# Delta-rule scan inside a decoder layer: key norms by a power on GpSimd, the output added by ScalarE and GpSimd, and another order of TensorE's work in each chunk

## What is computed

```python
proj = normed @ w_qkvb + b_qkvb
q, k, v, beta_pre = jnp.split(proj, 4, axis=-1)
beta = jax.nn.sigmoid(beta_pre)
# 16 heads of 16 features each
k = k / jnp.maximum(jnp.linalg.norm(k, axis=-1, keepdims=True), NORM_EPS)

def step(S, inp):
    q_t, k_t, v_t, beta_t = inp
    retrieval = jnp.einsum('bhij,bhj->bhi', S, k_t)
    S = S + jnp.einsum('bhi,bhj->bhij', beta_t * (v_t - retrieval), k_t)
    o_t = jnp.einsum('bhij,bhj->bhi', S, q_t)
    return (S, o_t)
_, out_t = lax.scan(step, S0, (q, k, v, beta))
return x + scan_out @ w_out + b_out
```

## Time and profile before

| | us |
|---|---|
| median of 3 runs | 1056.92 |
| the profiled execution | 1053.93 |
| its span in the profile | 1052.0 |
| PE busy | 909.3 (86%) |
| DVE busy | 876.4 (83%) |
| ACT busy | 656.4 (62%) |
| POOL busy | 516.5 (49%) |
| mean granted clock of TensorE | 0.937 of 2.4 GHz |

### The profile page before, as it was taken

The page is one execution under the profiler, slowest core; times in us unless marked ns, Lnnn a source line. Parts: engine busy times, 40 slices in busy tenths (PEclk is TensorE's granted clock), DMA queues, the critical chain, the costliest instruction groups (busy, mean ns, idle before and its releaser), DMA issues.

```text
span 1052.0 us, 19448 instructions
## 1 busy us (share of the span) xinstructions
PE 909.3 (86%) x6084; PEld 693.0 (66%) x6091; DVE 876.4 (83%) x2581; ACT 656.4 (62%) x1597; POOL 516.5 (49%) x753
## 2 busy tenths in 40 slices
PE   8799999999999999999999998989999901895066
PEld 7577787778778887877877877656666600442044
DVE  4789899989999999999999998865666657799887
ACT  4575777756667667666666665456777731894085
POOL 5344345433554563554355454236899980870000
PEclk9899999989999999999999999999999965898579
DMA  9700000000000000002100000132310000000012
GB/s 162 134 5 7 6 7 11 8 6 7 10 8 7 7 11 6 6 12 79 54 10 8 6 7 11 26 131 77 105 61 1 1 0 1 1 1 1 1 65 96
DMA packets 28573, 30.49 MB, mean 29 GB/s; under 512 B 5548, under 2 KB 23864, under 8 KB 28472
## 3 DMA queue, kind: packets, MB, share of 16 engines
q1 hardware_dynamic: 28256, 29.12, 11.0%
q10 hardware_dynamic: 216, 0.14, 0.0%
HBM read 20.85 MB, written 4.19 MB: 24 GB/s over the span
## 4 chain that ended last, share of the span: by engine, by line
PE 64%; DVE 17%; POOL 12%; issue 4%; ACT 1%; DMA 1%; SPq 1%; DVEq 0%; POOLq 0%; ACTq 0%
PE ps L1871 8%; PE ps L1863 7%; PE psG L1825 6%; PE ps L1802 5%; PE psY L1839 5%; PE psX L1839 4%; PE psX L1917 3%; PE psY L1917 3%; PE psG L1819 3%; PE ps L1931 2%; PE ps L2172 2%; PE psG L1820 2%; POOL arena L577 2%; POOL arena L575 2%; POOL xs L568 2%
## 5 line engine op out<-in xcount | busy, mean ns | idle before, releaser
L543 POOL TENSOR_TENSOR arena<-arena 128x256 f32<-128x256 f32 x32 | 23.3, 729 | 303.6 <-DVE arena L1206 303.6
L677 ACT ACTIVATE arena<-ps 128x512 f32<-128x512 f32 x128 | 72.9, 596 | 40.7 <-PE ps L1863 40.3
L1863 PE MATMUL ps<-work 32*128 32x256 f32 x512 | 94.2, 409 | 2.5 <-ACT work L723 1.8
L502 POOL TENSOR_SCALAR_AFFINE_SELECT arena<-arena 128x2048 f32<-128x2048 f32 x32 | 92.1, 2877 | 2.2
L642 ACT ACTIVATE arena<-ps,nparity 32x256 f32<-32x256 f32 x124 | 51.1, 458 | 48.3 <-PE ps L1802 47.9
L1863 PEld LDWEIGHTS ps<-work 32*128 32x128 f32 x512 | 62.7, 188 | 19.8 <-issue 12.0
L1825 PE MATMUL psG<-arena 128*128 128x512 f32 x128 | 74.0, 664 | 0.4 <-DVE arena L1272 0.4
L1217 DVE TENSOR_TENSOR arena<-arena 128x256 f32<-128x256 f32 (+1 forms) x96 | 66.6, 694 | 3.5
L1220 DVE TENSOR_REDUCE arena<-arena 128x64 f32<-128x256 f32 (+1 forms) x96 | 65.9, 686 | 3.3
L1802 PE MATMUL ps<-work,arena 128*128 128x64 f32 x496 | 61.5, 279 | 7.9 <-DVE work L1232 7.9
L1839 PEld LDWEIGHTS psY<-work,arena 128*128 128x128 f32 x512 | 59.8, 195 | 12.5 <-DVE arena L1289 10.7
(11 more groups left out here) (337 smaller groups left out, 2597.0 us busy)
## 6 DMA issues: line engine op xcount, KB each, us to landing
arena<-in_mask_BxSxS_ik SPq DMA_DIRECT2D x8, 1024.0 KB, 6.8
xs<-arena SPq DMA_DIRECT2D x256, 16.0 KB, 1.8
arena<-in_ctx SPq DMA_DIRECT2D x8, 512.0 KB, 4.4
out<-xs SPq DMA_DIRECT2D x32, 128.0 KB, 1.7
arena<-in_x SPq DMA_DIRECT2D x8, 288.0 KB, 17.9
arena<-in_L_ffn_w SPq DMA_DIRECT2D x2, 1024.0 KB, 21.9
arena<-in_x SPq DMA_DIRECT2D x16, 96.0 KB, 6.6
arena<-in_L_attn_w_qkvb SPq DMA_DIRECT2D x2, 512.0 KB, 5.2
```

The source lines that it names most:

```text
L502: G.affine_select(out=pairs, in_=pairs, compare_op=ALU.is_ge, fill=0.0, base=0, pattern=[[0, NH], [-CT, B], [0, CT]], channel_multiplier=1 ...
L677: A.activation(attn[j % 2][:, r * 512:(r + 1) * 512], ps[(2, 0)[r % 2]][:, :], ACT.Copy).then_inc(att_out, 1)
L1863: last = M.matmul(ps[(2, 0)[r % 2]][:, f * 2 * P:(f + 1) * 2 * P], kq[j % 4][rows, f * P:(f + 1) * P], qe[rows, f].rearrange("p e t -> p ( ...
```

## The change

1. VectorE's `key_norms` goes. ScalarE copies the sums of squares from PSUM to SBUF with the sign turned (`key_sums_out`), and GpSimd takes the maximum with the floor, raises it to the power -0.5 (`ALU.pow`, 128x16) and spreads it over the head's features with a copy.
2. VectorE's `x_added` goes. ScalarE copies the output projection from PSUM (`mixed_copied`, semaphore `mixed_out`), and GpSimd adds it to the chunk's input (`x_added`), after the masks and ahead of the norms. TensorE's waits for `x_done` become waits for `mixed_out`.
3. In `outputs` the loop over r, the strips of 32 columns, becomes the innermost.
4. TensorE's turn has a new order between the turned updates and the queries, as the last part of the diff shows.

```diff
-                ss, root, sqr = nrm
-                for n in range(3):
-                    own(G.tensor_tensor(sqr, root, root, ALU.mult))
-                    own(G.tensor_tensor(sqr, sqr, ss, ALU.mult))
-                    own(G.tensor_scalar(sqr, sqr, -0.5, 1.5, ALU.mult, ALU.add))
-                    if n < 2:
-                        own(G.tensor_tensor(root, root, sqr, ALU.mult))
+                ss, root, length = nrm
+                own(G.tensor_scalar(length, ss, NORM_EPS * NORM_EPS, None, ALU.max))
+                own(G.tensor_tensor(root, length, half, ALU.pow))
                 pool.wait_ge(rn_T, m)
-                wide = [t.rearrange("p (h a) -> p h a", a=1).broadcast_to([P, NH, HD]) for t in (sqr, root)]
-                G.tensor_tensor(rn_wide.rearrange("p (h d) -> p h d", d=HD), wide[0], wide[1], ALU.mult).then_inc(rn_ready, 1)
+                G.tensor_copy(rn_wide.rearrange("p (h d) -> p h d", d=HD),
+                              root.rearrange("p (h a) -> p h a", a=1).broadcast_to([P, NH, HD])).then_inc(rn_ready, 1)
+
+            def x_added(j):
+
+                pool.wait_ge(mixed_out, j + 1)
+                pool.wait_ge(xb_ready, j + 1)
+                G.tensor_tensor(xc[:, j, :], xc[:, j, :], mixed_s, ALU.add).then_inc(x_done, 1)
...
                 mask_attention(j)
+                if j >= 1:
+                    x_added(j - 1)
                 if j + 3 < NCK:
                     key_norms(j + 3)
...
+            def key_sums_out(m):
+
+                act.wait_ge(n_mm, m + 1)
+                act.wait_ge(rn_ready, m)
+                A.activation(nrm[0], ps[1][:, 0:NH], ACT.Copy, scale=-1.0).then_inc(seeded, 1)
+
+            def mixed_copied(j):
+
+                act.wait_ge(w_mm, j + 1)
+                act.wait_ge(x_done, j)
+                A.activation(mixed_s, ps[2][:, 0:D], ACT.Copy).then_inc(mixed_out, 1)
...
                     keys(m)
+                if exists(j - 1):
+                    mixed_copied(j - 1)
+                if exists(m):
+                    key_sums_out(m)
...
-            def key_norms(m):
-
-                v.wait_ge(n_mm, m + 1)
-                v.wait_ge(rn_ready, m)
-                ss, root, _ = nrm
-                squares, half = ps[1][:, 0:NH], ps[1][:, NH:2 * NH]
-                own(V.tensor_scalar(squares, squares, -1.0, NORM_EPS * NORM_EPS, ALU.mult, ALU.max))
-                own.issue(V.tensor_copy(ss, squares))
-                own(V.tensor_scalar(half.bitcast(I32), squares.bitcast(I32), 1, None, ALU.logical_shift_right))
-                own(V.tensor_scalar(root.bitcast(I32), half.bitcast(I32), -1.0, SEED, ALU.mult, ALU.add))
-                v.sem_inc(seeded, 1)
...
-            def x_added(j):
-                v.wait_ge(w_mm, j + 1)
-                v.wait_ge(xb_ready, j + 1)
-                V.tensor_tensor(xc[:, j, :], xc[:, j, :], ps[2][:, 0:D], ALU.add).then_inc(x_done, 1)
...
                     if j >= 1:
-                        pe.wait_ge(x_done, j - 1)
+                        pe.wait_ge(mixed_out, j - 1)
...
-                for r in range(4):
-                    for f in range(DC):
-                        for e in range(2):
+                for f in range(DC):
+                    for e in range(2):
+                        for r in range(4):
...
-                for f in range(2):
-                    if exists(j):
-                        attention(j, 2 * f)
-                        attention(j, 2 * f + 1)
-                    if exists(j + 1) and j >= 1:
-                        far_gram(j + 1, f)
-                    if f == 0 and exists(j + 2) and j >= 1:
-                        norms_turned(j + 2)
+                if exists(j + 1) and j >= 1:
+                    far_gram(j + 1, 0)
+                if exists(j):
+                    attention(j, 0)
+                    attention(j, 1)
+                if exists(j - 1):
+                    outputs(j - 1)
+                if exists(j):
+                    attention(j, 2)
+                    attention(j, 3)
+                if exists(j + 1) and j >= 1:
+                    far_gram(j + 1, 1)
+                if exists(j + 2) and j >= 1:
+                    norms_turned(j + 2)
                 if j == 0:
                     far_gram(1, 0)
                     far_gram(1, 1)
-                if exists(j - 1):
-                    outputs(j - 1)
```

More of the change, by code:

```diff
@@ L157, in decoder @@
         variances, newton = sums_of[:, 0:2, :], sums_of[:, 2:4, :]
-        half = sb("half", [P, B])[:, :]
+        half = sb("half", [P, NH])[:, :]
         w1q = sb("w1q", [P, FC, D], BF16)
@@ L213, in decoder @@
         nT += [take(D).rearrange("p (c t) -> p c t", c=DC) for _ in range(2)]
+        mixed_s = take(D)
         assert at[0] <= ARENA - NT * D, at[0]
@@ L358, in decoder @@
         yn_ready, hr_ready, hs_ready, tok_mm, picked, cand_ready = [sem(n) for n in "yn_ready hr_ready hs_ready tok_mm picked cand_ready".split()]
+        mixed_out = sem("mixed_out")
         last_known, att_moments, hid_moments, last_moments = [
@@ L532, in row_norms @@
                 own(G.tensor_scalar(qr[:, cols], s2[:, cols], 1.0 / D, LN_EPS, ALU.mult, ALU.add))
-                own(G.tensor_tensor(qr[:, cols], qr[:, cols], half, ALU.pow))
+                own(G.tensor_tensor(qr[:, cols], qr[:, cols], half[:, 0:B], ALU.pow))
                 G.tensor_tensor(qs[:, cols], qs[:, cols], qr[:, cols], ALU.mult).then_inc(q_known, 1)
@@ L551, in _ @@
                         bounded_weights(p)
+            x_added(NCK - 1)
             def beta_added(n):
@@ L938, in _ @@
                     scaled_by_feature(1)
+                    key_sums_out(0)
                 else:
                     normed_x(2 * m)
+                    key_sums_out(m)
                     scaled_by_feature(m + 1)
@@ L1178, in ternary_factors @@
                 v.wait_ge(abs_sum, 1)
+                v.wait_ge(seeded, 15)
                 own(V.tensor_reduce(wsum[:, :], ps[1][:, 32:40].rearrange("p (k n) -> p k n", k=2), AX.X, ALU.add))
@@ L1415, in _ @@
             input_stats(1)
-            key_norms(0)
             input_sums(1)
@@ L1421, in _ @@
             input_factors(1, input_total(1), -0.5)
-            key_norms(1)
             keys_normed(0)
@@ L1431, in _ @@
                 if j == 0:
-                    solve(0, {2: ((key_norms, 2),), 4: ((keys_normed, 1), (far_products, 1)), 8: ((near_products, 1),),
+                    solve(0, {4: ((keys_normed, 1), (far_products, 1)), 8: ((near_products, 1),),
                               12: ((keys_normed, 2),)})
@@ L1445, in _ @@
                     least(1)
-                if exists(j - 1):
-                    x_added(j - 1)
                 if exists(j + 1) and j + 1 < NCK - 1:
@@ L1451, in _ @@
                     state(j + 1)
-                if exists(j + 3):
-                    key_norms(j + 3)
                 if j == 11:
@@ L1928, in mixed @@
                 pe.wait_ge(oT_ready, j + 1)
-                pe.wait_ge(x_done, j)
+                pe.wait_ge(mixed_out, j)
                 for c in range(DC):
@@ L1947, in context_whole @@
                 else:
-                    pe.wait_ge(x_done, NCK - 1)
+                    pe.wait_ge(mixed_out, NCK - 1)
                 for u in range(NW):
@@ L1990, in probabilities @@
                 if n == 1:
-                    pe.wait_ge(x_done, NCK)
+                    pe.wait_ge(mixed_out, NCK)
                 elif n >= 2:
```

## The result

The changed kernel takes 1158.78 us (median of 4 runs, 1158.48 to 1159.43) where the kernel before takes 1056.02 in the same comparison: a ratio of 1.098, 95% interval 1.096 to 1.100. It is 10% slower. The forecast was 1147, slower.

A forecast was written before the change was run, and what follows sets the result against it. VectorE's ring and TensorE's order, nearly equal, were taken to hold the scan's 20.22 us turn. From 1053.93 us, +45.9 (wait for norms) and -1.3 gave 1098.5, +48.6 (slow clock) gave 1147; range 1090 to 1178.

The forecast's parts named there:

- What bounds the kernel: Scan loop over 32 chunks: VectorE's ring and TensorE's order of work, nearly equal, hold a turn of 20.22 us.
- VectorE's ring: Scan turn: VectorE's turned updates release the state's matmuls, then L1289, the retrieval, L1315 and the solve to the next updates.
- Part 1: Key norms and output addition leave VectorE: its ring gains 0.66 us a turn; ScalarE, GpSimd, prologue and tail cost nothing.
- Rival D: GpSimd's power takes over 6 us and becomes what L1228 waits for: 1150 us and up; chance 0.03.
- Part 2: TensorE's new order: turned norms end at 560.28 instead of 557.54, VectorE waits, a turn grows 1.70 us, +45.9 in 27 turns.
- rival C: TensorE's column groups don't run side by side, outputs stay 2.46 us: +34 us on top, 1132 or 1181; chance 0.08.
- Part 3: TensorE idles some 3.4 us ahead of every state, its clock halves: 1.8 us in each of 27 turns, +48.6.
- Rival B: VectorE's wait for the norms comes, but TensorE's clock stays at 2.4 GHz in most turns: about 1098 us; chance 0.16.
- The sum: Whole kernel: 1053.93 us plus 45.9 for the wait, less 1.3, gives 1098.5; plus 48.6 for the slow clock, 1147.
- Rival E: L1228 on VectorE isn't delayed; the ring gives 0.66 us in 31 turns, -20, so 1034 us; chance 0.05.

The follow-up runs named there:

- the moved work alone: Changed kernel with TensorE's order and the outputs' loop of the kernel before, so only key norms and output addition moved: 1049.14 us, ratio 0.994.
- the experiment on the tail: Changed kernel with GpSimd's addition of chunk 30 ahead of the masks of chunk 31 instead of behind them: 1151.07 us.
- the filled run: Changed kernel with 12 added 128x128 matmuls, read by nobody, ahead of every chunk's state on TensorE: 1096.44 us, ratio 1.039.
- the early norms: Changed kernel with TensorE turning the norms of chunk j + 2 right behind attention 0 and 1, ahead of the outputs: 1061.89 us, ratio 1.006.

## Why the prediction was right, and where it was off

**What bounds the kernel.** Right. Two chains of nearly equal length: with the moved work alone TensorE holds the turn at 20.2 us, with TensorE's order also relieved VectorE's ring goes to 19.66. The ring's gain of 0.66 us had been worked out, and 20.22 - 0.66 = 19.56 is 0.1 from what ran.

**Part 1.** Right in its terms. GpSimd in the turn shown above (L524 the addition, L515 the power, L517 the spread):

```profile
553.96 0.72 POOL L524 TENSOR_TENSOR arena<-arena 128x256 f32<-128x256 f32 x1
554.65 0.25 POOL L514 TENSOR_SCALAR work<-work 128x16 f32<-128x16 f32 x1
554.98 2.93 POOL L515 TENSOR_TENSOR work<-work,half 128x16 f32<-128x16 f32 x1
557.98 0.77 POOL L517 COPY work<-work 128x256 f32<-128x256 f32 x1
```

The power took 2.93 us (2.9 taken), and all ended at 557.98 + 0.77 = 558.75, while TensorE turned the norms at 564.11. Rival D falls. What was wrong is "The prologue and the tail change by less than 1 each way": for the tail I counted the added hop of the last addition, and not that the addition of the chunk before it now stood behind 5 us of masks in GpSimd's queue, nor that its transfers stood ahead of the last ones in SyncE's. This term was 7.8 us instead of 0, and the experiment on the tail took back 6.9 of it. It is two thirds of the 12 us between 1147 and 1159.

**Part 2.** Right in the mechanism, a little too high in size: +1.53 us a turn at full clock, measured with the filled idle time, instead of 1.70. Up to L1254 my order was right as a whole: from the first Gram to L1254 the filled run takes 538.55 to 544.31, 5.76 us, where I had 554.54 to 560.33, 5.79. Its pieces were off both ways: from the Gram to attention 0.95 instead of 1.06, the outputs 1.01 instead of 1.2 (rival C falls), attention 2 and 3 1.28 instead of 1.07. I had made attention 2 wait for both of ScalarE's copies; by the kernel it needs only the first (in the turn shown after, it starts at 561.87, ahead of the copies' end at 562.04), and attention 3 alone waits for the second. So that the errors cancel is luck. Most of the missing 0.17 lies behind L1254: the next state starts 8.38 us behind it (544.31 to 552.69) and not 8.52, since in the kernel before TensorE's own full queue held the state back a little: there it started 0.91 us behind L1232's start, here 0.77 behind L1258's.

**Part 3.** Right in the mechanism: idle time of 3.44 us (3.4 forecast) ahead of most states, half a clock behind it. The size was 2.15 us a turn instead of the middle of 1.8. From the ninth turn to the twenty-ninth every turn has a fall of 6.8 us or more, the longer of the two kinds that the earlier trace rows show; it costs less than the 3.0 us read there, and in the turn shown 1.4 of its 6.8 us pass while TensorE waits anyway (547.7 to 549.1). Rival B falls: the granted clock did fall. Without the slow clock the kernel would take 1096, as the filled run shows, which is B's 1098.

**The sum.** As forecast, the wait stands in 27 of the 29 turns; in the other two, at 89.2 and 227.8 us, VectorE starts L1254 without waiting. The filled run's 29 turns took 637.7 us, and this splits the stretch: the wait cost 637.7 - 599.1 = 38.6 us (45.9 forecast), the slow clock 697.4 - 637.7 = 59.7 (48.6 forecast). Together 98.3 against 94.5, because two errors of opposite sign nearly cancel. With the other rows of the table, -2.6, +1.5 and +7.8, for which I had 0, -1.3 and 0, it makes 105.0 against 93.2.

**Rival E**, no delay of L1228, is what the early norms make of the kernel. Its 1034 counted the ring's gain in every turn and no slow clock; 1061.9 was measured, since a relieved TensorE stands idle and the clock falls behind part of its waits. It takes added work or the slower outputs to collect the ring's gain, and even then 1043.2 was the best: the 29 turns gave 12.8 us back and the stretch behind them took 5.3.

## What to carry to other kernels

Before moving a producer in an in-order queue, look up where its consumer stands in its own queue, and compare the two times: here 1.09 us of slack in one row said that a step could be moved by one matmul group, not by four. When work moves to another engine, follow its last pass through every queue behind it: masks ahead of it on GpSimd and other transfers ahead of it on SyncE cost 7 us here that no turn of the loop shows. And where TensorE shares a ring with another engine, time saved on it beyond the ring's length is no gain and can be a loss by its clock: give it something to do, or leave it its slower loop.

## What the runs showed of the hardware that I had not expected

- 32 instructions of matmuls that fill strips of 32 columns took 1.08 us when each went to the next strip in turn, and 2.46 when all of one strip came before the next.
- Idle times of TensorE ahead of the state's matmuls, and the half clock: with 0.2 to 0.86 us it never came in these profiles; with 0.9 to 1.5 us it came in some turns and not in others of the same kernel, for 3.4 or 6.8 us (early norms: behind 0.90 at 317.3 and 1.39 at 519.8, not behind 1.02 at 297.6); with 2.0 to 2.6 us in most but not all (changed kernel: not behind 2.34 at 121.9 and 214.0); with 2.9 us and more in every turn.
- The slow clock hits the state's and the near Gram's matmuls in full (1.90 to 3.68 us; first part of the near Gram, from start to start, 0.92 to 1.82).
- Twelve matmuls a turn whose result nobody reads made the changed kernel 62 us faster.
- A power of 128x16 elements on GpSimd took 2.93 us, where 128x8 took 1.66.
